# Paired tails of experts, projections by products of parts, and a later load of shared weights, in a two-layer float32 stack on one core

## The chip, the core and the metric

The kernel runs on one core of a Trainium2 chip. Such a core has a matrix engine (TensorE, PE in the profile, with its weight loads shown apart as PEld), three engines for elementwise work (VectorE or DVE, ScalarE or ACT, GpSimd or POOL), and SyncE (SP), which here only issues transfers. Each engine takes its own instructions in order; they wait for one another through semaphores. Data lies in SBUF (128 partitions) and PSUM (eight banks of 128 x 512 floats, into which TensorE writes). The metric is the device time of one execution in microseconds (us); lower is better.

## The reference

The reference is six blocks, each added to its input: windowed self-attention, cross-attention, a mixture of 64 experts with a shared expert, a state-space mixer, a second cross-attention and a dense layer with low-rank experts. There are 8 sequences of 256 tokens, width 512. The change touches the first three blocks. What matters of them:

```python
# self-attention: 16 heads, a window of 64 keys; its last step is the output projection
out = out.transpose(0, 2, 1, 3).reshape(B, S, EMB)
return out @ w_out.T
...
# cross-attention: its last projection, before a layernorm of the delta
ctx = ctx.transpose(0, 2, 1, 3).reshape(B, S, H)
delta = _nan_clean(ctx @ Wo.T + bo)
...
# experts: 192 places each; buf holds the rows routed to an expert
buf = jnp.zeros((E * C, H), x.dtype).at[slot].set(x[tok]).reshape(E, C, H)
g = jnp.einsum('ech,emh->ecm', buf, Wg)
u = jnp.einsum('ech,emh->ecm', buf, Wu)
out = jnp.einsum('ecm,ehm->ech', jax.nn.silu(g) * u, Wd).reshape(E * C, H)
...
shared = jax.nn.silu(x @ Sg.T) * (x @ Su.T) @ Sd.T
```

## The kernel before

Everything is written out by hand: each stage is a block in which every engine has its own program, and the order of the code is the order of the work. Waits are for constants of counts. There are four stages in a row: `phase1` (both attentions of the first layer, sequence by sequence), `shared_expert` (the shared expert, the router and the scatter of tokens into expert slots), `phase2` (the 64 experts), and then the second layer (`mixers`, `lora_ffn`), which the change leaves alone but for two semaphores that are taken from a reused range.

Two ways of multiplying float32 stand side by side. Either TensorE takes float32 operands directly (`project_pe`, L188), or each operand is first split into a high part, rounded to the format fp32r by an ACT copy, and a low part, the rest, by a DVE subtraction; the product is then the sum of three products of parts, high by high, high by low and low by high (`PRODUCTS`, issued by `products`, L730, in `phase1` and by L328 and L1797 for the experts).

**`phase1`.** Eight sequences, i from 0 to 7, one after the other; `last` is 7. For a sequence PE first projects queries and keys in eight chunks and the values (L730, `w_slot`), then runs the local heads (L780 to L822). DVE divides each chunk of 128 channels of attended values by its row sums into `oT` (`divide`, L1002), after ACT has copied the reciprocals (`copy_recips`, L626). PE covers the end of that with half of the cross values (`cross_values(0)`), multiplies `oT` by `w_out` in float32 (8 instructions of 128 x 512: two blocks j of 128 rows by four chunks; every one shows as two records in the trace), and goes on with `cross_values(1)`. DVE adds the result to the input (`residual`, L1007) and takes the statistics of the layernorm. In the cross-attention the divided values come as two halves (L1109), after two ACT copies (L711); PE covers these with the keys of the next sequence (`keys(i + 1, (3,))`) and then multiplies by `w_xo`, again in float32. DVE takes the two blocks of the delta (`take_delta`, L971) and turns at once to the rotary step (`rope`, L959 to L962) of the next sequence, which PE awaits before its first local scores (L780). The tiles `w_sg`, `w_su`, `w_sd` and `hr0` at the right end of SBUF hold raw pieces of projection weights in sequence 0 and are then free until the shared expert's weights are loaded into them, in sequence 2 (L524 to L532). In sequence 7 the splitting of those weights, the turning of the first rows of the next stage and its first products are laid between the cross-attention's steps (`shared_opening`, `shared_turn`, `shared_gate_up`).

**`phase2`.** For expert e PE runs gate and up (three chunks m of the 352 hidden channels, L328), turns the gathered rows of expert e + 1 (`turn_expert`, L302), and then multiplies down (L1797: for each m three products, in the order aT_hi by wd_hi, aT_hi by wd_lo, aT_lo by wd_hi; L1801 for the last 64 rows in float32). The 192 rows of an expert are gathered as two tiles, 128 and 64 rows, by two indirect transfers of POOL, and both tiles are turned as full 128 x 128 blocks: eight transposes, half of the second four's output unused. ACT and DVE split the turned rows (L308, L314). For each m DVE makes the gated activation (L1854, L1858), its high part aT_hi (L1861) and its low part aT_lo (L1863); PE waits for aT_lo (`eact_ready`) before the first of the three products of that m. Buffers are in twos by the parity b of e, and the raw down weights in fours.

## Time and profile before

| | us |
|---|---|
| time, median of 3 runs | 3115.08 (3113.67 to 3115.29) |
| time of the profiled execution | 3110.33 |
| its span | 3108.5 |
| `phase1`, sequences 0 to 7 | 0 to about 759 |
| one sequence of it | 90 to 92 |
| `shared_expert` | about 760 to 1001 |
| `phase2` | about 1001 to 1771 |
| one expert, in the steady part | about 12.1 |
| second layer | from there to 3108.5 |

The profiled execution took 1.8 us more than its span, and 4.75 us less than the median of the three timed runs. Over the whole span PE is busy 95%, DVE 74%, ACT 51% and POOL 26% of the time. A PE record starts where its matmul begins to stream and is longer than the time until the next one starts, since matmuls overlap; so the cost of a group is read from its first start to the first start of what follows.

### The profile page before, as it was taken

Reading aid. Unit: us, or ns where it says so; the run is one execution under the profiler, and the core shown is the slowest. Engines: PE = TensorE matmul, PEld = TensorE weight load, DVE = VectorE, ACT = ScalarE, POOL = GpSimd, SP = SyncE. Lnnn points to the kernel's source line nnn. Section 1 sums busy time; section 2 is a strip of 40 time slices with the busy share of each in tenths; the row PEclk is TensorE's granted clock in tenths of the full one; section 3 lists DMA queues with packets and bytes.
Section 4 is the critical chain, followed back from the end, with each engine's and each line's share of the span. In section 5 each row is a group of like instructions: output and inputs, shape, how many; then the busy total and the mean of one; then the engine's idle time right before and its main releaser. Section 6 shows DMA issues by size and latency. Waiting matters only on the chain. (4 is left out here: it accounts for less than half of the span.)

```text
span 3108.5 us, 61772 instructions
## 1 busy us (share of the span) xinstructions
PE 2954.8 (95%) x23073; PEld 2384.2 (77%) x23073; DVE 2301.0 (74%) x4321; ACT 1579.0 (51%) x3643; POOL 808.7 (26%) x974
## 2 busy tenths in 40 slices
PE   7999999998999999999999969999999989999999
PEld 5666666665998888888888846767676678888888
DVE  5665666665876788888888668878786887777776
ACT  3323333333222555555555436666666765555554
POOL 1221122122664111111111073342412022222222
PEclk9999999999999999999999989999999999999999
DMA  7324333330312777777777642221210032222222
GB/s 281 116 93 188 126 140 112 126 113 29 119 56 65 235 244 248 236 249 237 250 244 243 229 142 65 69 73 56 69 42 18 33 125 75 76 79 80 76 69 72
DMA packets 146539, 403.96 MB, mean 130 GB/s; under 512 B 39488, under 2 KB 48192, under 8 KB 133520
## 3 DMA queue, kind: packets, MB, share of 16 engines
q1 hardware_dynamic: 107888, 325.36, 30.8%
q0 software_dynamic: 18976, 50.45, 5.7%
q10 hardware_dynamic: 19456, 25.18, 2.4%
q8 instruction: 143, 2.34, 0.3%
q14 instruction: 76, 0.62, 0.1%
HBM read 344.06 MB, written 54.76 MB: 128 GB/s over the span
## 5 line engine op out<-in xcount | busy, mean ns | idle before, releaser
L288 POOL DMA_INDIRECT hr<-normed_rows,idx x128 | 124.4, 972 | 629.2 <-PE psum L302 593.0
L3018 POOL TENSOR_TENSOR mixf<-act 128x256 f32<-128x256 f32 x128 | 143.2, 1119 | 458.6 <-DVE act L3284 458.6
L174 POOL TENSOR_SCALAR ve<-mv 128x1 f32<-128x1 f32 x112 | 35.9, 321 | 762.7 <-DVE mv L967 505.5
L328 PE MATMUL psum<-xT_hi,wgu_hi 128*128 128x192 f32 (+1 forms) x1536 | 228.4, 271 | 1.5 <-PEq L1127 0.9
L328 PE MATMUL psum<-xT_hi,wgu_lo 128*128 128x192 f32 (+1 forms) x1536 | 223.3, 268 | 0.0
L328 PE MATMUL psum<-xT_lo,wgu_hi 128*128 128x192 f32 (+1 forms) x1536 | 223.1, 268 | 0.0
L1744 ACT ACTIVATE eth<-psum 128x192 f32<-128x192 f32 (+1 forms) x192 | 63.2, 330 | 300.2 <-PE psum L328 293.5
L328 PEld LDWEIGHTS psum<-xT_hi,wgu_hi 128*128 128x128 f32 (+1 forms) x1536 | 190.3, 182 | 26.7 <-ACT wgu_hi L1728 21.5
L2312 ACT ACTIVATE scratch<-psum,smin 128x512 f32<-128x512 f32 x256 | 173.7, 687 | 62.3 <-DVE smin L2758 60.6
L328 PEld LDWEIGHTS psum<-xT_lo,wgu_hi 128*128 128x128 f32 (+1 forms) x1536 | 190.7, 183 | 0.0
L328 PEld LDWEIGHTS psum<-xT_hi,wgu_lo 128*128 128x128 f32 (+1 forms) x1536 | 190.5, 183 | 0.0
L3284 DVE TENSOR_TENSOR act<-act,maskT 128x512 f32<-128x512 f32 x128 | 88.1, 689 | 116.7 <-ACT act L3060 116.3
L2758 DVE TENSOR_REDUCE smin<-psum 128x2 f32<-128x1024 f32 x128 | 155.2, 1215 | 25.3 <-PE psum L2489 24.5
L2499 PEld LDWEIGHTS psum<-ident,scratch 128*128 128x128 f32 x1024 | 109.2, 141 | 59.0 <-issue 37.7
L2499 PE MATMUL psum<-ident,scratch 128*128 128x128 f32 x1024 | 145.3, 281 | 7.5 <-DVE scratch L2765 3.9
L1854 DVE SCALAR_TENSOR_TENSOR eact<-eth,psum 128x192 f32<-128x192 f32 (+1 forms) x192 | 67.5, 352 | 113.2 <-ACT eth L1744 110.8
L3294 DVE TENSOR_TENSOR ca_lo<-act,ca_hi 128x512 fp32r<-128x512 f32 x128 | 134.3, 1049 | 12.4
L730 PE MATMUL psum<-hT_hi,w_slot 128*128 128x256 f32 x768 | 110.8, 289 | 11.9 <-ACT hT_hi L607 5.9
L1267 POOL DMA_INDIRECT slot_token<-tok_i,slot_w x96 | 103.4, 1077 | 66.5 <-DVE slot_r L1592 41.6
L1098 DVE TENSOR_SCALAR arena<-psum,hi 128x512 f32<-128x512 f32 x128 | 87.5, 745 | 42.9 <-PE psum L836 42.9
L2126 POOL DMA_INDIRECT yk<-expert_out,slots x84 | 86.3, 1028 | 119.8 <-issue 48.4
L3073 ACT ACTIVATE ca_hi<-act 128x512 fp32r<-128x512 f32 x128 | 81.0, 633 | 66.5 <-DVE act L3284 66.5
(466 smaller groups left out, 8644.4 us busy)
## 6 DMA issues: line engine op xcount, KB each, us to landing
w_sg<-in_w_gu_dram SPq DMA_DIRECT2D x32, 1408.0 KB, 6.0
w_su<-in_w_gu_dram SPq DMA_DIRECT2D x32, 1408.0 KB, 5.9
w_slot<-w_split SPq DMA_DIRECT2D x21, 2048.0 KB, 8.9
w_raw<-in_w_dram SPq DMA_DIRECT2D x128, 256.0 KB, 2.6
w_sd<-in_w_d_dram SPq DMA_DIRECT2D x32, 512.0 KB, 8.7
wd<-in_w_d_dram SPq DMA_DIRECT2D x32, 512.0 KB, 8.6
expert_out<-so ACTq DMA_DIRECT2D x64, 256.0 KB, 5.3
w_slot<-w_split SPq DMA_DIRECT2D x28, 512.0 KB, 5.0
```

Source lines behind the costliest of these rows:

```text
L288: pool.indirect_dma_start(out=xg[0:w, t, :], out_offset=None, in_=rows, in_offset=bass.IndirectOffsetOnAxis(ap=idx[0:w, t:t + 1], axis=0)) ...
L328: ins = pe.matmul(bank(2 + m)[0:w, gu * CAP:(gu + 1) * CAP], wgu2[wp][:, gu, kc, m0:m0 + w], xT2[xp][:, kc, :], start=(i == 0 and kc == 0) ...
L730: ins = pe.matmul(out, lhs_of(lp, kc), rhs_of(rp, kc), start=(m == 0 and kc == 0), stop=(m == 2 and kc == KC - 1))
L1098: dve.tensor_scalar(xprobs[:, n % 4, kt], bank_pair(2 * (n % 2))[:, :, kt * S:(kt + 1) * S], hi[:, kt:kt + 1], -SCORE_CLIP * ROOT_HD, ALU. ...
L1267: pool.indirect_dma_start(out=dr["slot_token"], out_offset=bass.IndirectOffsetOnAxis(ap=slot_w[s % 2][:, j, k:k + 1], axis=0), in_=tok_i[s ...
L2126: pool.indirect_dma_start(out=gathered(s, NT * k + j), out_offset=None, in_=dr["expert_out"], in_offset=bass.IndirectOffsetOnAxis(ap=slots ...
L2312: act.activation(prob[:, q % 4, k, :], bank_pair(2 * (q % 2))[:, k, :], ACT.Exp, bias=smin[b][:, n, k:k + 1], scale=-1.0, accum_out=ssum[b ...
L2499: ins = pe.transpose(bank(4 + k)[:, mc * P:(mc + 1) * P], prob[:, q % 4, k, mc * P:(mc + 1) * P], ident)
L2758: dve.tensor_reduce(smin[(q // PAIRS) % 2][:, q % PAIRS, :], bank_pair(2 * (q % 2)), AX.X, ALU.min).then_inc(sy["smin_ready"], 1)
L3018: pool.tensor_tensor(mixf[:, g % LAG, :], act2[:, g % LAG, 0, :], act2[:, g % LAG, 1, :], ALU.add).then_inc(sy["f_mix"], 1)
L3284: dve.tensor_tensor(act2[:, g % LAG], act2[:, g % LAG], maskT[(g // FC) % 2][:, 2:4, :], ALU.mult).then_inc(sy["f_ca"], 1)
L3294: dve.tensor_tensor(ca2[1][:, g % LAG], act2[:, g % LAG], ca2[0][:, g % LAG].bitcast(F32), ALU.subtract).then_inc(sy["f_ca_lo"], 1)
```

## The change

Three things change.

First, in the experts: an even expert e now gathers, as its second tile, its own last 64 rows and the last 64 rows of expert e + 1 (`load_slots`, `gather_expert`), and turns eight blocks; the odd expert gathers and turns only its first 128 rows, four blocks, and takes its last 64 from the half of bank 1 that its neighbour's turn left (`turned_tiles`). The down products wait for the high part before the first product of an m and for the low part only before the third.

Second, in sequences 1 to 6 of `phase1`: both output projections are done by products of parts. `w_out` and `w_xo` are split once, at the end of sequence 0, into tiles laid over `w_su`, `w_sd`, `hr0` and part of `w_sg`; `oT` is split for each projection by ACT (`attended_hi`, `crossed_hi`) and DVE (`low_part`) into tiles laid over `qk`. Sequences 0 and 7 stay in float32.

Third, since the split weights occupy the room, the shared expert's weights and its first rows are loaded in sequence 7, behind the load of the cross queries' weights.

```diff
 def load_slots(sp, sy, dr, idx, e, b):
-    sp.dma_start(idx[0:CAP - P, 1:2], slot_token[bass.ds(e * CAP + P, CAP - P)]).then_inc(sy[f"idx_in{b}"], 16)
+    for half in range(0 if b else 2):
+        sp.dma_start(idx[half * SMALL:(half + 1) * SMALL, 1:2],
+                     slot_token[bass.ds((e + half) * CAP + P, SMALL)]).then_inc(sy[f"idx_in{b}"], 16)
...
 def gather_expert(pool, sy, dr, xg, idx, b):
-    for t, (c0, w) in enumerate(C_TILES):
+    for t in range(1 if b else 2):
         pool.indirect_dma_start(
-            out=xg[0:w, t, :], out_offset=None, in_=rows,
-            in_offset=bass.IndirectOffsetOnAxis(ap=idx[0:w, t:t + 1], axis=0)).then_inc(sy[f"xg_in{b}"], 16)
+            out=xg[:, t, :], out_offset=None, in_=rows,
+            in_offset=bass.IndirectOffsetOnAxis(ap=idx[:, t:t + 1], axis=0)).then_inc(sy[f"xg_in{b}"], 16)
...
+def turned_tiles(bank, b):
+
+    tiles = [bank(t)[:, :].rearrange("p (c t) -> p c t", c=KC) for t in range(2)]
+    return (slice(0, P), tiles[0]), (slice(P, CAP), tiles[1][:, :, b * SMALL:(b + 1) * SMALL])
+
+def turn_expert(pe, sy, ident, bank, xg, b):
+    for t in range(1 if b else 2):
+        for kc in range(KC):
+            ins = pe.transpose(bank(t)[:, kc * P:(kc + 1) * P], xg[:, t, kc * P:(kc + 1) * P], ident)
     ins.then_inc(sy["exT_psum"], 1)
...
+        OUT_PARTS, XO_PARTS = ((0, 2), (2, 3), (3, 4)), ((0, 2), (2, 4))
+        def in_parts(i):
+
+            return 0 < i < last
...
-                if i == 2:
-                    sp.wait_ge(sy["rows_out"], i * 32)
+                else:
+                    sp.wait_ge(sy["delta_psum"], due("delta_psum", i - 1, NT))
+                    sp.wait_ge(sy["rows_out"], (i - 1) * 32)
+                    for n in ("w_sg", "w_su"):
+                        sp.dma_start(held[n][:], dr[n]).then_inc(sy["shared_in"], 16)
                     sp.dma_start(held["hr0"][:], dr["normed_rows"][0].rearrange("(t p) d -> p t d", p=P)
                                  ).then_inc(sy["shared_in"], 16)
...
+            def out_weights_hi(n, half):
+                act.wait_ge(sy["w_lo"], split_done(XQ, KC - 1))
+                kcs = slice(2 * half, 2 * half + 2)
+                act.activation(w_o2[n][0][:, kcs, :], W_RAW[n][:, kcs, :], ACT.Copy).then_inc(sy["w_hi"], 1)
...
                 copy_recips(i, 2)
+                if in_parts(i):
+                    attended_hi(i, 0)
                 copy_recips(i, 3)
+                if in_parts(i):
+                    attended_hi(i, 1)
+                    attended_hi(i, 2)
...
+                if in_parts(i):
+                    for part in range(len(XO_PARTS)):
+                        crossed_hi(i, part)
                 if i < last:
                     keys_copy(i + 1, 3, KC)
...
+            def out_products(out, n, j, first, end):
+
+                return products(out[:, :], lambda p, kc: oT2[p][:, kc, j * P:(j + 1) * P],
+                                lambda p, kc: w_o2[n][p][:, kc, :], PRODUCTS, first, end)
...
+                if in_parts(i):
+                    pe.wait_ge(sy["w_lo"], split_done(XQ, KC - 1) + 4)
+                    pe.wait_ge(sy["oT_hi"], xo_part(i, len(XO_PARTS)))
+                    for j in range(NT):
+                        out_products(bank(6 + j), "xo", j, 0, 2)
+                        if j == 0:
+                            pe.wait_ge(sy["oT_lo"], xo_part(i, len(XO_PARTS)))
+                        out_products(bank(6 + j), "xo", j, 2, 3).then_inc(sy["delta_psum"], 1)
...
+            def low_part(count, c0, end):
+                dve.wait_ge(sy["oT_hi"], count)
+                dve.tensor_tensor(oT2[1][:, c0:end, :], oT[:, c0:end, :], oT2[0][:, c0:end, :].bitcast(F32), ALU.subtract
+                                  ).then_inc(sy["oT_lo"], 1)
...
+                if i == 0:
+                    for k in range(4):
+                        out_weights_lo(k, ("out", "xo")[k // 2], k % 2)
...
                 for m in range(NM):
-                    pe.wait_ge(sy["eact_ready"], e * NM + (m + 1))
+                    pe.wait_ge(sy["ehi_ready"], e * NM + (m + 1))
                     for i, (ap, wp) in enumerate(PRODUCTS):
+                        if ap:
+                            pe.wait_ge(sy["eact_ready"], e * NM + (m + 1))
                         pe.matmul(bank(5)[:, :], aT2[b][ap][:, m, 0:P], wd2[b][wp][:, m, :],
                                   start=(m == 0 and i == 0), stop=(m == NM - 1 and i == 2))
```

How this stands in the program, in three places. In the lists `x8` means eight alike in a row, and the waits of an instruction stand behind it.

PE at the end of sequence 1 of `phase1`, before: the keys of the next sequence (ctxT by w_xk), the projection (w_xo), and the first queries of sequence 2.

```order
L188 MATMUL psum<-ctxT,w_xk 128x256 [waits colsT_lo]
L188 MATMUL psum<-ctxT,w_xk 128x256 x3
L188 MATMUL psum<-w_xo,oT 128x512 [waits xattn_ready]
L188 MATMUL psum<-w_xo,oT 128x512 x7
L730 MATMUL psum<-hT_hi,w_slot_76 128x256 [waits slot_a,xk_ready,colsT_lo]
```

PE at the same place now.

```order
L187 MATMUL psum<-ctxT,w_xk 128x256 x3
L788 MATMUL psum<-w_xo_hi,oT_hi 128x512 [waits oT_hi,w_lo]
L788 MATMUL psum<-w_xo_hi,oT_hi 128x512 x3
L788 MATMUL psum<-w_xo_lo,oT_hi 128x512 x4
L788 MATMUL psum<-w_xo_hi,oT_lo 128x512 [waits oT_lo]
L788 MATMUL psum<-w_xo_hi,oT_lo 128x512 x3
L788 MATMUL psum<-w_xo_hi,oT_hi 128x512 x4
L788 MATMUL psum<-w_xo_lo,oT_hi 128x512 x4
L788 MATMUL psum<-w_xo_hi,oT_lo 128x512 x4
L788 MATMUL psum<-hT_hi,w_slot_80 128x256 [waits slot_a,xk_ready,colsT_lo]
```

Eight float32 instructions have become 24 of parts; the first now waits for ACT's copy of `oT` and the ninth for DVE's low part.

ACT over the cross-attention's end in sequence 1, before: xkT is the copy of keys, cosq and sinq take the spread reciprocals.

```order
L615 ACTIVATE xkT<-psum,bk 128x256 [waits xk_psum]
L711 ACTIVATE cosq<-psum 128x512 [waits xrecT_psum]
L711 ACTIVATE sinq<-psum 128x512 [waits xrecT_psum]
L615 ACTIVATE xkT<-psum,bk 128x256 [waits xk_psum]
L663 ACTIVATE arena<-psum 128x256 [waits qk_proj] x8
```

ACT at the same place now.

```order
L646 ACTIVATE xkT<-psum,bk 128x256 [waits xk_psum]
L762 ACTIVATE cosq<-psum 128x512 [waits xrecT_psum]
L762 ACTIVATE sinq<-psum 128x512 [waits xrecT_psum]
L673 ACTIVATE oT_hi<-oT 128x512 [waits xattn_ready] x2
L646 ACTIVATE xkT<-psum,bk 128x256 [waits xk_psum]
L709 ACTIVATE arena<-psum 128x256 [waits qk_proj] x8
```

The two copies of `oT` stand between the copy of the second reciprocals and that of the last keys.

PE in `phase2`, within an even expert, between its gate and up products and the rest of its down products, before: hr is the odd neighbour's gathered rows.

```order
L302 MATMUL psum<-ident,hr_85 128x128 [waits exT_lo,xg_in1]
L302 MATMUL psum<-ident,hr_85 128x128 x7
L1797 MATMUL psum<-wd_hi_96,aT_hi_108 128x512 [waits eact_ready,eout_ready,wd_lo]
L1797 MATMUL psum<-wd_lo_97,aT_hi_108 128x512
L1797 MATMUL psum<-wd_hi_96,aT_lo 128x512
L1797 MATMUL psum<-wd_hi_96,aT_hi_108 128x512 [waits eact_ready]
```

PE at the same place now.

```order
L316 MATMUL psum<-ident,hr_89 128x128 [waits exT_lo,xg_in1]
L316 MATMUL psum<-ident,hr_89 128x128 x3
L1900 MATMUL psum<-wd_hi_100,aT_hi_112 128x512 [waits ehi_ready,eout_ready,wd_lo]
L1900 MATMUL psum<-wd_lo_101,aT_hi_112 128x512
L1900 MATMUL psum<-wd_hi_100,aT_lo 128x512 [waits eact_ready]
L1900 MATMUL psum<-wd_hi_100,aT_hi_112 128x512 [waits ehi_ready]
```

Four of the eight transposes are gone at this one of the two places in a pair of experts, and the wait for the low part stands two products later.

## Rows read from the trace of the kernel before

**Rows 1.** The page's part 1: busy time, share of the span, instructions.

```profile
PE 2954.8 (95%) x23073; PEld 2384.2 (77%) x23073; DVE 2301.0 (74%) x4321; ACT 1579.0 (51%) x3643; POOL 808.7 (26%) x974
```

**Rows 2.** Busy time and granted clock in five stretches; columns in the first row.

```profile
core 0: us, PE busy (x) PEld busy (x) DVE busy (x) ACT busy (x) POOL busy (x), PEclk, DMA share, GB/s
...
322.00:327.00 5.00, 5.00 (x25) 3.60 (x22) 2.53 (x5) 2.90 (x16) 0.00 (x0) 0.66 0.33 124
...
392.00:483.00 91.00, 87.04 (x716) 59.41 (x715) 58.01 (x100) 32.57 (x100) 18.07 (x25) 1.00 0.33 119
...
727.00:736.00 9.00, 8.47 (x65) 4.48 (x66) 5.53 (x9) 6.68 (x9) 1.27 (x1) 0.62 0.00 0
...
1040.00:1766.00 726.00, 726.00 (x6061) 644.49 (x6060) 593.26 (x1081) 403.69 (x660) 112.54 (x118) 1.00 0.75 248
```

**Rows 3.** PE's timeline, sequence 3: start, length, instruction, [idle before].

```profile
346.52 7.03 PE L188 MATMUL psum<-w_out,oT 128*128 128x512 f32 x16
353.39 3.60 PE L188 MATMUL psum<-w_xv,ctxT 128*128 128x512 f32 x8
...
389.20 7.03 PE L188 MATMUL psum<-w_xo,oT 128*128 128x512 f32 x16
395.66 1.50 PE L730 MATMUL psum<-hT_hi,w_slot 128*128 128x256 f32 x8
```

**Rows 4.** PE's timeline, sequence 7: values of one block as products of parts.

```profile
683.25 2.13 PE L730 MATMUL psum<-w_slot,hT_hi 128*128 128x512 f32 x8
...
686.16 0.39 PE L780 MATMUL psum<-wmask_b,ident_b 128*128 128x256 bf16 x2
```

**Rows 5.** DVE's timeline, sequence 3, then durations of splits (min/median/max ns).

```profile
343.70 0.43 DVE L1002 TENSOR_TENSOR oT<-psum,rec 128x256 f32<-128x256 f32 x1 [0.75 <-ACT rec L626]
...
388.30 0.69 DVE L1109 TENSOR_TENSOR oT<-psum,sinq 128x512 f32<-128x512 f32 x1 [0.17 <-ACT sinq L711]
...
396.27 0.75 DVE L971 SCALAR_TENSOR_TENSOR so<-psum,rs,rs_bo 128x512 f32<-128x512 f32 x1 [1.74 <-PE psum L188]
...
L632 ACT ACTIVATE sg_hi<-w_sg x6: 406/615/622, 728.3 to 751.6; 128x512 fp32r<-128x512 f32 x5, 128x256 fp32r<-128x256 f32 x1
L1019 DVE TENSOR_TENSOR sg_lo<-w_sg,sg_hi x6: 421/686/691, 728.9 to 756.4; 128x512 fp32r<-128x512 f32 x5, 128x256 fp32r<-128x256 f32 x1
```

**Rows 6.** End of sequence 0 on ACT and DVE, and splits of 128 x 1024.

```profile
118.39 0.47 ACT L615 ACTIVATE xkT<-psum,bk 128x256 f32<-128x256 f32 x1 [1.13 <-PE psum L188]
...
125.25 0.75 DVE L971 SCALAR_TENSOR_TENSOR so<-psum,rs,rs_bo 128x512 f32<-128x512 f32 x1 [1.74 <-PE psum L188]
...
L1734 ACT ACTIVATE wd_hi<-wd x32: 1049/1052/1056, 1020.1 to 1760.9; 128x1024 fp32r<-128x1024 f32 x32
...
L1831 DVE TENSOR_TENSOR wd_lo<-wd,wd_hi x32: 1224/1226/1228, 1021.7 to 1762.5; 128x1024 fp32r<-128x1024 f32 x32
```

**Rows 7.** One expert's turn and down products: PE's timeline, then DVE's.

```profile
1511.18 1.04 PE L302 MATMUL psum<-ident,hr 128*128 128x128 f32 x8
1511.98 0.48 PE L1797 MATMUL psum<-wd_hi,aT_hi 128*128 128x512 f32 x1
...
1513.46 0.39 PE L1797 MATMUL psum<-wd_hi,aT_hi 128*128 128x512 f32 x1
...
1512.51 0.26 DVE L1861 CAST aT_hi<-eact 96x192 fp32r<-96x192 f32 x1
1512.80 0.35 DVE L1863 TENSOR_TENSOR aT_lo<-eact,aT_hi 96x192 fp32r<-96x192 f32 x1
```

**Rows 8.** PE's waits from 1000 to 1050: us in total, times, longest.

```profile
PE psum L1797 <- DVE aT_lo L1863: 3.6, 4, 1.6
```

**Rows 9.** Transfers: shared weights' time to land, SP and PE in sequence 7.

```profile
w_sd<-in_w_sd_dram SPq DMA_DIRECT2D x1, 128.0 KB, 18.2
...
688.45 0.59 SPq L473 DMA_DIRECT2D w_slot<-w_split  x1
...
725.72 0.66 PE L182 MATMUL psum<-ident,hr 128*128 128x128 f32 x4
```

More of the change, by code:

```diff
@@ L213, in shared_weights @@
     tiles = {n: right(n, shape) for n, shape in shapes.items()}
+    at = nc.sbuf_top
+    tiles["w_o2"] = {n: [nc.alloc_sbuf_tensor_at(f"w_{n}_{part}", [P, KC, D], F32R, offset=at + 4 * (2 * i + j) * KC * D)
+                         for j, part in enumerate(("hi", "lo"))] for i, n in enumerate(("xo", "out"))}
     tiles["w_gate"] = ctx.enter_context(nc.sbuf_tensor("w_gate", [P, KC, E], F32))
@@ L362, in phase1 @@
         wmask = arena[:, 2048:2048 + S]
+        qk_at = nc.sbuf_base
         qk = sb("qk", [P, 2 * KC, S])
+        oT2 = [nc.alloc_sbuf_tensor_at(f"oT_{part}", [P, KC, S], F32R, offset=qk_at + 4 * j * KC * S)
+               for j, part in enumerate(("hi", "lo"))]
         xkT = sb("xkT", [P, KC, S])
@@ L716, in _ @@
                     shared_chunks_hi(4, len(MS_CHUNKS))
+                if i == 0:
+                    for n in ("out", "xo"):
+                        for half in range(2):
+                            out_weights_hi(n, half)
             sy.end_turn(act, 0, 0)
@@ L1073, in _ @@
                 divide(i, 2)
+                if in_parts(i):
+                    low_part(out_part(i, 1), *OUT_PARTS[0])
                 divide(i, 3)
+                if in_parts(i):
+                    for part in (1, 2):
+                        low_part(out_part(i, part + 1), *OUT_PARTS[part])
                 if i == 0:
@@ L1111, in _ @@
                                       ALU.mult).then_inc(sy["xattn_ready"], 1)
+                if in_parts(i):
+                    for part in range(len(XO_PARTS)):
+                        low_part(xo_part(i, part + 1), *XO_PARTS[part])
+                if i == 0:
+                    for k in range(4):
+                        out_weights_lo(k, ("out", "xo")[k // 2], k % 2)
             for at in range(4, 9):
@@ L1634, in _ @@
             dve.wait_ge(sy["exT_hi"], 1)
-            turned_lo(dve, sy, bank, first["xT2"])
+            turned_lo(dve, sy, bank, first["xT2"], 0)
             out(nseq - 1)
```

121 lines of the change are left out of this document (71 added, 50 removed).

## The prediction

> **What bounds the kernel now.** I read the busy shares first [rows 1]: PE is busy 95% of the span, DVE 74%, ACT 51%. Then the busy time by stretches [rows 2], since such a share is a mean over stages. In the steady part of the experts PE is busy 726.0 of 726 us at full clock: every TensorE instruction taken out there counts, unless a wait takes its place. In a sequence of `phase1` (392 to 483 is sequence 4) PE is busy 87 of 91 us, and there the question is what it waits for after the edit. So the third view is PE's timeline around the projections and the turn [rows 3, 4, 7], beside DVE's and ACT's at the same moments [rows 5 to 7]. I cost each edit as a change of PE's time, and then look at whether its inputs would come in time.
>
> **The local output projection, sequences 1 to 6.** Before, w_out takes from 346.52 to 353.39, 6.87 us, for 8 float32 instructions (16 records) [rows 3]. The same shape as products of parts is there in the values: 12 products, from 683.25 to 686.16, 2.91 us [rows 4]. The new projection has 24 of them, 5.82 us, so it saves 1.05. Its inputs: the last chunk of oT is ready at 343.70 + 0.43 = 344.13 [rows 5]; ACT copies it as 128 x 256 (0.41, the shortest of the sg_hi copies), DVE subtracts (0.42) [rows 5], and both are done by about 345.1, while PE comes there at 346.52. The first low part is issued between two divisions, where DVE idled 0.75 us [rows 5], about its own length. DVE and ACT have nothing to do until the first block of the projection is out, so nothing waits behind these splits. The second block is out 1.05 earlier, and the layernorm and the turning that hang on it move along. 6 x 1.05 = 6.3 us.
>
> **The cross projection, same sequences.** The same 1.05 is saved: w_xo's records are as long and as many as w_out's [rows 3]; its next start comes after 6.46 and not 6.87, but the group that starts there is stretched to 1.50 us, and I take it that the missing 0.4 is in it. Here the inputs are late. The second half of oT ends at 388.30 + 0.69 = 388.99, and PE starts at 389.20. Now ACT's copy of 128 x 512 stands between, 0.615 us [rows 5]. With 0.1 for two hand-overs, my allowance, PE starts at 389.7, 0.5 late. Bounds of that: 0.4 with no hand-overs, and 0.8 with two of 0.2, which is what DVE takes after PE (396.27 against 389.20 + 6.87). I take 0.5, since the shorter hand-overs are those between ACT and DVE. DVE's second low part would end at about 390.4, PE needs it after eight products, at 391.6: hidden. Queued behind ACT's new copies is only the copy of the last keys, for which PE asks after the projection; behind DVE's is the delta, not out before 392.6. The second delta block is out at 395.5 and not at 396.1, so both PE's queries and DVE's long run through layernorm and rotation, for which PE waits before the local scores, start 0.55 earlier. 6 x 0.55 = 3.3 us, within 1.5 and 3.9.
>
> At this place a rule of the Trainium skill stands against the row. The row has a float32 instruction of 512 columns at 6.87 / 8 = 0.86 us and a product of parts at 2.91 / 12 = 0.243 [rows 3, 4]. The Trainium skill (FP8 and Floating Point Precision, section TensorE Precision Notes) says that true float32 takes four passes through the array, and reduced precision is a matter of one read and truncation; by that rule three products would take three quarters of 6.87, and the saving would be 1.72 and not 1.05. The trace agrees with the four passes only in part, since its product is 13% dearer than a quarter of 0.86; the rule's own time is among the rivals.
>
> **Splitting the two weights, once, end of sequence 0.** ACT is free from 118.39 + 0.47 = 118.9 and makes four copies of 128 x 1024, 1.05 each, until 123.1; its next work comes after that. DVE follows with four subtractions of 1.23, from about 119.9 to 124.8 [rows 6]. They stand before the delta in its queue. The first block (about 1.6 us with its statistics) then ends near 126.4, and the second starts there and not at 125.25 [rows 6]: 1.2 us late, and it is that run for which PE waits before the scores. Cost 1.2 us, once; between 0 (if its slack takes it) and 1.5.
>
> **The turn of the experts.** Eight transposes take from 1511.18 to 1511.98, 0.80 us [rows 7]. The 32 turns of odd experts keep four, so each saves 0.40. That the products behind can start earlier needs their inputs. The third m's first product, at 1513.46, would stand at 1513.06. Its high part is ready at 1512.51 + 0.26 = 1512.77; its low part at 1512.80 + 0.35 = 1513.15, too late for the old wait, and in time for the new one, since the third product comes two products later, near 1513.5. DVE's work up to there starts from the gate's results and is not moved. Extra waits that are already met should cost nothing. 32 x 0.40 = 12.8 us. From below 0.25 a turn, 8.0 us, if PE can start the third m only as if the low part were still asked for (the distance from 1513.21, the low part with a hand-over, to 1513.46); from above 0.45, 14.4 us, as the group's own length of 1.04 hints. The even turns have as many transposes as before. ACT's and DVE's splits keep their 768 columns, cut as 512 and 256. POOL has 32 gathers less, of the same rows in all.
>
> **The opening of the experts.** SP issues a third index transfer ahead of expert 2's weights, about 0.5 us, and PE's four waits for low parts, 3.6 us [rows 8], may each shrink by up to 0.35 through the later wait. I take 0, within 1.5 either way.
>
> **The shared weights.** In sequence 2 they stood, as they will in sequence 7, right behind a load of 2 MB of projection weights, and the last of them landed 18.2 us after its issue. In sequence 7 they can be issued from 689.0 on, so they are there by about 709 to 711; PE turns their first rows at 725.72 [rows 9]. Some 15 us to spare, cost nothing. If that cover were gone the delay would come whole onto the path, since PE and ACT both wait for them. Taking them out of sequence 2 gives nothing that I can see.
>
> **The clock.** The granted clock is 1.00 in sequence 4 and in the experts; from 322 to 327, in sequence 3, it is 0.66 and from 727 to 736, in sequence 7, 0.62, that is, 1.2 GHz for most of these stretches [rows 2]. These cost 5 x 0.34 = 1.7 and 9 x 0.38 = 3.4 us. Sequence 4 has the same work as sequence 3, leaves PE idle for 4 us too and stays at 1.00, so I can't say where dips will fall in the new kernel. I allow 4 us either way and take 0.
>
> **Sum.** 6.3 + 3.3 - 1.2 + 12.8 = 21.2 us less. The profiled execution, 3110.33, would be 3089.1. It stood 4.75 below the median of the timed runs, so for the median I take 3115.08 - 21.2 = **3093.9 us**.
>
> **The rivals.**
> - *The down products still wait at the short turns.* For it: only 0.3 us lie between the high part and the new start. Against: DVE's chain is that early by the row. The turn then saves 8.0: 3098.7 us. 10%.
> - *The cross projection gains nothing,* because ACT and DVE come later than in my one sequence, or the 0.5 us spreads. 3115.1 - 17.9 = 3097.2 us. 10%.
> - *The dips of the clock go.* For it: they look like chance. Five us more gain: 3088.8 us. 10%.
> - *Three quarters,* the float32 pass's share and nothing for the weight loads. 12 x 0.67 = 8.0 us more: 3085.9 us. The values' row speaks against it. It is the rule named above. 4%.
> - *The turn is hidden,* that is, the experts are paced by arriving weights or by DVE (82% busy there), and only `phase1` gains, 8.4: 3106.7 us. Against: PE's 726.0 of 726. 4%.
> - *Slower.* The new wait before each cross projection and the shorter, denser local one bring a low clock after them, as after the light stretches of rows 2, at 3.4 us each. With all twelve: 40.8 - 21.2 = 19.6 us more, 3134.7 us. It decides from seven of the twelve on (21.2 / 3.4 = 6.2). Against: sequence 4 has 4 us of waits already and no dip [rows 2]. 4%.
>
> **How the numbers follow.** My forecast has 58%, with 3090 to 3097 as its own range. The range for 8 in 10 takes in the first three rivals and most of the unknown costs, and leaves out the last three (12%) and the tails: 3087 to 3102. A measurement of this kernel tells about 0.2%, 6.2 us, from no change. Faster by more than that is everything below 3108.9: all but the slow rival and a few per cent around the hidden turn, 93%; within it 3%; slower 4%.
>
> **What would show it.** In the new profile: the span from w_out's first start to the cross values behind it is 5.8 us; PE idles about 0.5 us before w_xo, put down to ACT, in sequences 1 to 6 only; the short turn takes 0.40 and a pair of experts 23.8 and not 24.2 us, with no wait for the high or the low part behind it; PE's wait before sequence 1's scores is about 1.2 us longer; nothing waits for the shared weights in sequence 7. Wrong would be: PE idle before the down products of even experts, an idle of 1 us or more before w_xo, the wait for `qk` before the scores longer by what the projections save, or new stretches of clock under 0.7.

## The result, and the profile after

The changed kernel takes 3093.92 us (median of 5 runs, 3090.02 to 3101.35) where the kernel before, beside it on the same chip, takes 3115.08 (5 runs, 3113.67 to 3116.58): a ratio of 0.9933, 95% interval 0.9917 to 0.9949. Measured again beside the experiments it took 3088.78 us against 3112.29, a ratio of 0.9927 (0.9915 to 0.9939). The forecast was 3093.9.

So the total is right. That the first median meets it to a tenth is luck: its five executions spread over 11 us, and the second median is 5 us lower. Its parts are not all right, and that is what the rest is about. The profiled execution took 3093.92 us, span 3092.2, which is 16.4 less than the profiled execution of before, where the sum said 21.2. The changed kernel's page, part 1, to be read beside [rows 1]:

```profile
PE 2935.5 (95%) x23041; PEld 2391.8 (77%) x23041; DVE 2315.3 (75%) x4355; ACT 1597.6 (52%) x3677; POOL 779.7 (25%) x940
```

Five stretches of the changed kernel in the view that [rows 2] has of before; the number behind POOL's is the granted clock:

```profile
core 0: us, PE busy (x) PEld busy (x) DVE busy (x) ACT busy (x) POOL busy (x), PEclk, DMA share, GB/s
142.50:149.30 6.80, 6.80 (x26) 4.59 (x26) 2.84 (x5) 3.00 (x17) 0.00 (x0) 0.50 0.41 155
...
323.50:326.90 3.40, 3.40 (x15) 2.49 (x11) 2.23 (x5) 2.65 (x15) 0.00 (x0) 0.51 0.09 31
422.40:432.60 10.20, 9.92 (x94) 6.66 (x94) 3.50 (x7) 4.06 (x22) 0.00 (x0) 0.50 0.77 326
497.00:588.00 91.00, 86.59 (x757) 64.81 (x755) 63.25 (x111) 35.74 (x107) 20.70 (x31) 1.00 0.35 127
1040.00:1750.00 710.00, 709.88 (x5907) 627.46 (x5907) 583.50 (x1074) 399.97 (x656) 85.41 (x87) 1.00 0.74 252
```

The experts are as they were, full clock and PE busy throughout, only shorter. In sequences 1 to 6 of `phase1` there are now stretches at 1.2 GHz (a granted clock of 0.50) in sequences 1, 2, 3 and 4, 23.9 us together with the 3.4 us from 234.7; before there was one, 3.4 us in sequence 3.

The undisturbed sequence 5 of the changed kernel on PE, for [rows 3], from its first scores to the queries of the next sequence:

```profile
504.46 0.38 PE L843 MATMUL psum<-wmask_b,ident_b 128*128 128x256 bf16 x2 [0.82 <-DVE qk L1044]
...
525.75 3.60 PE L187 MATMUL psum<-w_xv,ctxT 128*128 128x512 f32 x8
528.79 1.49 PE L788 MATMUL psum<-w_out_hi,oT_hi 128*128 128x512 f32 x4
...
534.76 3.59 PE L187 MATMUL psum<-w_xv,ctxT 128*128 128x512 f32 x8
538.19 1.04 PE L181 MATMUL psum<-ident,so 128*128 128x128 f32 x8
...
568.85 1.89 PE L187 MATMUL psum<-ctxT,w_xk 128*128 128x256 f32 x8
571.18 1.17 PE L788 MATMUL psum<-w_xo_hi,oT_hi 128*128 128x512 f32 x4 [0.44 <-ACT oT_hi L673]
...
576.83 1.10 PE L788 MATMUL psum<-hT_hi,w_slot 128*128 128x256 f32 x8
```

The eight float32 instructions of `w_xv` take 3.43 us for half a projection (534.76 to 538.19), so the local projection starts at 525.75 + 3.43 = 529.18 and lasts until 534.76: 5.58 us, 0.2325 a product. (Its first record already starts at 528.79, but the next one comes only 0.63 us later. Both groups together take 9.01 us, and took 10.30 before, so the saving doesn't hang on where the border is laid.) The cross projection takes 5.65 and starts 0.60 late (571.18, where the keys would have let it start at 568.85 + 1.73 = 570.58). From the first cross values of sequence 5 to those of sequence 6 it is 87.92 us; before, 89.81.

A short turn and the down products behind it, for [rows 7], and the first long turn after it:

```profile
1510.56 0.60 PE L316 MATMUL psum<-ident,hr 128*128 128x128 f32 x4
1510.92 0.48 PE L1900 MATMUL psum<-wd_hi,aT_hi 128*128 128x512 f32 x1
...
1512.39 0.40 PE L1900 MATMUL psum<-wd_hi,aT_hi 128*128 128x512 f32 x1
...
1513.18 1.51 PE L1904 MATMUL psum<-wd,eact 128*64 128x256 f32 x12
...
1522.22 1.03 PE L316 MATMUL psum<-ident,hr 128*128 128x128 f32 x8
1523.02 0.48 PE L1900 MATMUL psum<-wd_hi,aT_hi 128*128 128x512 f32 x1
```

The short turn takes 0.36 us, the long one 0.80, and nothing waits behind these two. At others something does: between 1100 and 1700 us PE's weight loads wait 13 times for the high part, up to 0.5 us.

```profile
PEld psum L1900 <- DVE aT_hi L1964: 3.9, 13, 0.5
```

PE's waits from 140 to 700 us (us in total, times, longest):

```profile
PE psum L843 <- DVE qk L1044: 7.7, 7, 2.8
...
PE psum L788 <- ACT oT_hi L673: 2.6, 6, 0.4
...
PE psum L877 <- DMA v_mid<-v: 1.2, 1, 1.2
```

The wait of 2.8 us before the scores is that of sequence 1, behind the splitting of the weights; its six others are 0.4 to 1.2 us, as in the kernel before. The wait for `v_mid`, the shifted values, is in sequence 4, and its long stretch of low clock begins at 422.44, at the end of that wait (PE's timeline):

```profile
422.68 0.66 PE L877 MATMUL psum<-arena,v 128*32 128x128 f32 x8 [1.22 <-DMA v_mid<-v]
```

Where the 16.4 us lie, by the starts of the same instruction in both profiles: 1.3 us before the first cross projection, where nothing was changed; 0.8 from there to the router's first product (645.28 and 644.48 us); 0.1 in `shared_expert`; 15.0 from the first expert's gate to the second layer (813.71 and 798.70 us); and 0.9 lost again in the second layer. So `phase1`, for which the sum had 8.4, gave almost nothing in this execution. Two things hide in it: the projections gave more than forecast, and the splitting of the weights and the low clock took it back.

### The profile page after: what moved, and what is told of

The parts are those of the page before. It is cut to its first block and busy times, and to the rows that moved or that the text cites. A ratio compares the mean times of both kernels' runs of the same rounds, so it can differ in the third digit from the quotient of the medians.

```text
span 3092.2 us, 61813 instructions
## 1 busy us (share of the span) xinstructions
PE 2935.5 (95%) x23041; PEld 2391.8 (77%) x23041; DVE 2315.3 (75%) x4355; ACT 1597.6 (52%) x3677; POOL 779.7 (25%) x940
## 5 line engine op out<-in xcount | busy, mean ns | idle before, releaser
L292 POOL DMA_INDIRECT hr<-normed_rows,idx x96 | 95.8, 998 | 642.3 <-PE psum L316 597.1
L3397 DVE TENSOR_TENSOR ca_lo<-act,ca_hi 128x512 fp32r<-128x512 f32 x128 | 134.2, 1048 | 12.5
```

Of the source, the lines that this page charges most:

```text
L292: pool.indirect_dma_start(out=xg[:, t, :], out_offset=None, in_=rows, in_offset=bass.IndirectOffsetOnAxis(ap=idx[:, t:t + 1], axis=0)).the ...
L3397: dve.tensor_tensor(ca2[1][:, g % LAG], act2[:, g % LAG], ca2[0][:, g % LAG].bitcast(F32), ALU.subtract).then_inc(sy["f_ca_lo"], 1)
```

## The experiments

All are read against the kernel before on the same chip. Since every kernel's time moved by several us with the mean granted clock of the execution, I also give the span that a straight line through all executions' spans against their mean clocks gives for a clock of 0.987. The line has one slope for all kernels, 2.3 us for each 0.001, and a height for each; single executions lie 1.4 us about it. Differences under 2 us between its values should not be leant on. "At equal clock" below means these values.

| kernel | median us | runs | ratio (95%) | mean clock | span at 0.987 |
|---|---|---|---|---|---|
| before | 3112.8 | 63 | | 0.9863 | 3109.3 |
| changed, both measurements | 3090.3 | 11 | 0.9933, 0.9927 | 0.9854 | 3086.4 |
| late_load | 3113.1 | 11 | 0.9999 (0.9991 to 1.0008) | 0.9858 | 3108.9 |
| late_wait | 3111.9 | 11 | 1.0000 (0.9991 to 1.0009) | 0.9862 | 3108.6 |
| parts_only | 3109.6 | 12 | 0.9992 (0.9983 to 1.0001) | 0.9845 | 3102.3 |
| tails_only | 3098.9 | 6 | 0.9951 (0.9938 to 0.9965) | 0.9868 | 3097.3 |
| xo_parts | 3101.6 | 5 | 0.9958 (0.9945 to 0.9971) | 0.9852 | 3095.1 |
| wout_parts | 3090.6 | 5 | 0.9923 (0.9910 to 0.9936) | 0.9868 | 3088.5 |
| old_wait | 3108.2 | 11 | 0.9983 (0.9974 to 0.9992) | 0.9839 | 3098.9 |
| filled | 3087.6 | 5 | 0.9920 (0.9907 to 0.9934) | 0.9880 | 3088.5 |
| split_later | 3094.8 | 5 | 0.9941 (0.9927 to 0.9954) | 0.9844 | 3087.5 |
| late_add | 3084.6 | 5 | 0.9907 (0.9894 to 0.9921) | 0.9866 | 3079.5 |
| v123 | 3077.1 | 4 | 0.9886 (0.9872 to 0.9901) | 0.9873 | 3076.3 |

In what follows a dip is a stretch of granted clock 0.50. My theory of the dips went through three forms, and the letters in the expectations change with it. In the first four, A is chance and B is that the denser projections and longer waits bring the dips. In the next ones A is what B was, narrowed to the cross projection, and C is chance. Last came the idle time before the scores.

**One part alone: tails_only.** The kernel before with the expert hunks of the diff.

> The kernel before with the experts' part of the change alone: paired tails, 32 short turns of four transposes, and the later wait for the low part. Both theories, the edits add up and only their sizes are open: in the profile of the changed kernel the short turn took 0.36 us and a pair of experts 23.78 to 23.86 us for 24.2 before, so 29 pairs of steady experts give some 11.5 us, and the opening of the experts 1.3 more through the later wait: 3115.1 - 13 = 3102. If the experts were paced by something else behind PE, under 5 us.

Measured 3098.87. At equal clock 12.0 us, where some 13 were expected. 56 intervals from turn to turn take 666.41 us in its profile against 677.76.

**The other part alone: parts_only.** The kernel before with all other hunks.

> The kernel before with both projections of sequences 1 to 6 by parts and the later load of shared weights, experts as before. Theory A, the dips of the clock fall by chance: a sequence without a dip takes 87.9 us for 89.8, so 6 x 1.9 - 1.7 for the splitting of the weights = 9.7 us less, 3105.4 us, and its mean clock is not lower than that of the kernel with the later load alone. Theory B, the denser projections and the longer waits bring the dips: the net gain is about 1 us as between the two profiles (dips 11.8 us in sequences 1 to 4 against 1.6), 3114 us, with a mean clock some 0.003 to 0.005 lower.

Measured 3109.56: between A and B, and not clear of no gain at all (the interval reaches 1.0001). At equal clock it gains 6.7 us on late_load, and its mean clock is lower by 0.0013, some 3 us.

Two things in it don't fit a plain sum. Its experts, whose code is that of before, take 679.65 us for the 56 intervals, 1.9 more than before and than late_load (677.73), and between 1100 and 1700 us PE's weight loads wait more often for the low part (in the kernel before it is 1.4 us in 8 waits):

```profile
PEld psum L1891 <- DVE aT_lo L1957: 4.1, 13, 0.6
```

And at equal clock the two parts give 12.0 and 7.0, where the whole change gives 22.9. Of the 3.9 us between, one lies in the experts, where the whole takes 0.9 us more than tails_only and not 1.9; the rest, some three times the uncertainty of this sum, is open.

**late_load.** As parts_only, with this edit and without the splitting of `w_out` and `w_xo`:

```diff
         def in_parts(i):
 
-            return 0 < i < last
+            return False
```

> The kernel before with only the load of the shared expert's weights and first rows moved from sequence 2 to sequence 7; projections in float32, experts as before. Expected by the sum: no cost, 3115.1 us within 1, and no wait for the shared weights. If the load is late or disturbs other transfers, 1 us or more slower. It also shows how often the clock dips in float32 sequences.

Measured 3113.11 against 3113.04. The later load costs nothing. Its profile has dips in sequences 3, 5 and 6: float32 sequences have them too.

**wout_parts.** The changed kernel with the cross projection in float32.

```diff
-                if in_parts(i):
+                if False:
                     pe.wait_ge(sy["w_lo"], split_done(XQ, KC - 1) + 4)
...
-                if in_parts(i):
-                    for part in range(len(XO_PARTS)):
-                        crossed_hi(i, part)
```

> The changed kernel with the cross projection in float32 again (w_xo's parts are still made, not used). Theory A: it loses what the cross projection gave, 6 x 0.62 = 3.7 us, 3097.6 us. Theory B, the wait for ACT's copy before w_xo and what follows it bring the dips: the loss is made up by fewer dips, 3094 us or less, with a mean clock above 0.986.

Measured 3090.59 at a mean clock of 0.9868: by its numbers that is theory B, and I took the dips for the cross projection's fault. An undisturbed sequence takes 88.54 us, so this projection gives 1.27 of the 89.81.

**after_again and xo_parts.** The changed kernel once more, and with the local projection in float32 instead.

> The changed kernel once more, beside the three below. From the runs so far, a line through spans against mean clocks puts it at 3087.0 us of span for a mean clock of 0.987, where the kernel before stands at 3109.3; its mean clock was 0.9846 in five executions, that of the kernel before 0.9861 in 23. Theory A (the cross projection by parts lowers the clock): again 0.9845 or so and 3094 us. Theory C (it was chance): a mean clock of 0.986 and 3090 us.

Measured 3088.78, clock 0.9860 in six executions. That is theory C's number, and the median, 1.8 us under that of wout_parts, is not told from it. So the low clock of the first five was in part chance. That all of it was is not shown.

> The changed kernel with the local projection in float32 again, the cross projection still by parts. At equal clock it should lose the local projection's gain, 6 x 1.29 = 7.7 us, and stand near 3094.7 us of span for a clock of 0.987. Theory A: its mean clock is as low as the changed kernel's, 0.9845, so the median is near 3102 us, slower than the experts' part alone (3098.9). Theory C: clock as in the kernel before, median near 3098.

Measured 3101.60 at a mean clock of 0.9852: the median is theory A's. An undisturbed sequence takes 89.24 us, so the cross projection gives 0.57; with 1.27 that makes 1.84 of the 1.89 that both give.

**late_add.** The changed kernel with DVE's additions moved off the path to the scores. GpSimd's matching work moves with them, and SP now loads the cross queries' weights and shifts the values before it stores the last sequence's rows; of these hunks only DVE's is shown:

```diff
                 for n in range(KC):
                     rope(i, n)
...
-                    if i >= 1 and n == 0:
+                    if i >= 1 and n == KC - 1:
                         for j in range(NT):
                             add_delta(i - 1, j)
```

> The changed kernel with VectorE's two additions of the normalised delta and their statistics (3.3 us) behind the fourth rotary step instead of the first, GpSimd's matching work and the store behind them too. PE's wait before the local scores (0.82 us in a sequence, 2.8 in sequence 1) should go: 6 to 8 us less at equal clock. Theory A in its form that this wait brings the dips: the mean clock rises from 0.9845 to 0.9865, 4 us more, about 3084 us. If the dips have another source: about 3087 us with the clock still at 0.9845. If the wait only moves to another place behind: 3092 or more.

Measured 3084.59, with 3079.5 at equal clock: 7 us better than the changed kernel. An undisturbed sequence takes 87.18, and in sequences 1 to 6 of the profile no dip is left. That profile is the fastest of five executions (3074.75 us, mean clock 0.989); the slowest had 0.984, so other executions had more low clock somewhere. Sequence 1, and sequences 2 to 6, of the changed kernel and then of late_add:

```profile
131.00:172.00 41.00, 36.74 (x331) 25.69 (x329) 27.36 (x53) 17.06 (x77) 6.61 (x10) 0.92 0.41 156
180.00:690.00 510.00, 484.13 (x4148) 359.17 (x4147) 345.40 (x590) 200.04 (x587) 106.68 (x146) 0.98 0.33 118
```

```profile
131.00:172.00 41.00, 39.00 (x358) 28.05 (x357) 29.67 (x58) 17.41 (x78) 8.42 (x13) 1.00 0.48 167
180.00:690.00 510.00, 489.13 (x4302) 360.80 (x4302) 349.03 (x604) 206.64 (x623) 96.75 (x142) 1.00 0.38 131
```

**filled.** late_add takes the wait away and DVE's chain with it. This one leaves the chain and fills PE's wait:

```diff
             def scores(i, n):
+                if i >= 1 and n == 0:
+                    for k in range(6):
+                        pe.matmul(bank_pair(0)[:, k % 2, 0:S], ident_b[:], wmask_b[:], start=True, stop=True)
```

> The changed kernel with six throwaway products (bf16, 128x256, about 0.16 us each) before PE's wait for the rotary step in sequences 1 to 7: they fill the 0.4 to 1.3 us of idle time there, and shorten nothing. If the idle time itself brings the dips of the clock in sequences 1 to 6, none is left there (the kernel that took the wait away had none, the changed kernel had four in one profile and two in the other): a sequence takes 87.9 to 88.1 us and the median is 2 to 4 us under the changed kernel's 3089 to 3094. If the dips come from something else that late_add took away, they stay at 2 to 4 and the median is the changed kernel's or up to 2 us above.

The six products are extra work, overwritten by what follows. Measured 3087.62, with the highest mean clock of all, 0.9880: its five executions have 0.987 to 0.989, the changed kernel's eleven 0.981 to 0.987. In time nothing is shown by that, since its ratio, 0.9920, lies within the changed kernel's intervals, and at equal clock it stands 2 us above the changed kernel. Its sequences 2 to 6 have no dip; sequence 1, where 1.81 us of wait remain in front of the scores, has one:

```profile
131.00:172.00 41.00, 37.51 (x339) 26.44 (x338) 27.79 (x52) 17.10 (x77) 7.22 (x10) 0.92 0.44 163
180.00:690.00 510.00, 488.13 (x4293) 362.84 (x4294) 350.47 (x600) 205.04 (x615) 106.68 (x146) 1.00 0.35 124
```

Over all profiles, sequences 2 to 6: with the wait before the scores in place there are 8 dips in 25 float32 cross projections (before 1, late_load 3, late_wait 2, tails_only 2, wout_parts 0) and 13 in 30 by parts; without it, or filled, 0 in 15. Of the 21, 19 begin 1.2 to 2.8 us after the first scores, and the other two, in sequence 4 of the changed kernel and sequence 3 of xo_parts, begin at the end of a wait of 1.2 us for `v_mid`. So PE's idle time goes with the dips. That it brings them is what filled speaks for, since it only fills the idle time; its profile alone (0 of 5 where the others have 21 of 55) would come by chance once in eleven times, and its clocks over five executions are the stronger evidence.

The projections by parts have a share in it that the count of dips doesn't show, 8 of 25 against 13 of 30. All 8 last 3.4 us; of the 13, five last 6.8 or 10.2. And over all executions changed, parts_only and xo_parts, which have the cross projection by parts and the wait before the scores, have a mean clock of 0.9850 in 28 executions (old_wait and split_later, lower still, add waits of their own). The five kernels with this projection in float32 have 0.9863 in 96, wout_parts with its 0.9868 among them; late_add, v123 and filled, which have the parts and not the wait, come to 0.9873 in 14. So parts and wait together go with 0.0013 less, some 3 us, four times its uncertainty. In what way the parts act is not shown.

**old_wait.** The changed kernel with the experts' wait where it was.

```diff
-                    pe.wait_ge(sy["ehi_ready"], e * NM + (m + 1))
+                    pe.wait_ge(sy["eact_ready"], e * NM + (m + 1))
                     for i, (ap, wp) in enumerate(PRODUCTS):
-                        if ap:
-                            pe.wait_ge(sy["eact_ready"], e * NM + (m + 1))
```

> The changed kernel with the experts' old wait: PE asks for the low part already before the first of the three products. By the rows of the kernel before, the low part is there 0.25 us after the point at which the short turn now ends earlier, so each of 32 short turns gives 0.25 and not 0.40: a pair of experts 23.95 us, some 4.5 us more than the changed kernel, with a wait for the low part behind each short turn. The rival: the low part comes in time at the short turns too and the later wait only helps in the opening: 1 us more.

Measured 3108.24, 12.5 us above the changed kernel at equal clock. The 56 intervals take 678.60 us: no less than the 677.76 of the kernel before, and 1.05 less than the 679.65 of parts_only, from which it differs by the paired tails alone (3 us at equal clock). PE's timeline at a short turn, and then DVE's at the third m:

```profile
1522.72 0.60 PE L316 MATMUL psum<-ident,hr 128*128 128x128 f32 x4
1523.08 0.48 PE L1898 MATMUL psum<-wd_hi,aT_hi 128*128 128x512 f32 x1
...
1524.32 0.40 PE L1898 MATMUL psum<-wd_hi,aT_lo 128*128 128x512 f32 x1
1524.74 0.50 PE L1898 MATMUL psum<-wd_hi,aT_hi 128*128 128x512 f32 x1
1525.08 0.40 PE L1898 MATMUL psum<-wd_lo,aT_hi 128*128 128x512 f32 x1
...
1525.64 0.66 PE L1902 MATMUL psum<-wd,eact 128*64 128x256 f32 x4
```

```profile
1524.34 0.35 DVE L1964 TENSOR_TENSOR aT_lo<-eact,aT_hi 96x192 fp32r<-96x192 f32 x1
```

The low part ends at 1524.69 and PE starts at 1524.74, 0.18 after 1524.32 + 0.24. Then the first product after the wait takes 0.34 to the next, and not 0.23. Both together are 0.29 of the 0.43 us that the turn saved, and waits at some long turns and longer pairs (up to 25.60 us) take the rest. Of the waits from 1040 to 1760 us most stand at PE's weight load and few at PE, so the list for PE alone would have shown a sixth of them:

```profile
PEld psum L1898 <- DVE aT_lo L1964: 19.7, 36, 1.3
...
PE psum L1898 <- DVE aT_lo L1964: 4.1, 14, 0.9
```

**late_wait.** The kernel before with only that wait moved.

> The kernel before with the later wait alone, eight transposes everywhere. No wait for the low part stands in the steady experts before, so nothing changes there: 24.2 us a pair. In the opening four waits sum to 3.6 us and may shrink by up to 0.35 each: 0 to 1.4 us less, within the measurement, 3112.

Measured 3111.93. The later wait gives nothing alone, and without it the short turns give 1 to 3 us: the gain is the pair's.

**split_later.** The changed kernel with the weights' low parts made by GpSimd in sequence 1.

```diff
-                if i == 0:
-                    for k in range(4):
-                        out_weights_lo(k, ("out", "xo")[k // 2], k % 2)
...
+                if i == 1:
+                    for k in range(4):
+                        pool.wait_ge(sy["w_hi"], split_done(XQ, KC - 1) + k + 1)
+                        n, kcs = ("out", "xo")[k // 2], slice(2 * (k % 2), 2 * (k % 2) + 2)
+                        pool.tensor_tensor(w_o2[n][1][:, kcs, :], W_RAW[n][:, kcs, :],
+                                           w_o2[n][0][:, kcs, :].bitcast(F32), ALU.subtract).then_inc(sy["w_lo"], 1)
```

> The changed kernel with one edit: the low parts of the two projection weights are made by GpSimd within sequence 1's heads, where it is idle, instead of by VectorE at the end of sequence 0. In the seven profiles so far that have this splitting on VectorE, PE waits 1.8 to 2.9 us before sequence 1's scores and the clock dips right behind it in every one, for 3.4 to 10.2 us; in the four without the splitting and in the two where the wait is gone it never does. Theory: the splitting's true price is the 1.7 us of the wait and 1.7 to 5.1 us of low clock behind it, so this kernel is 3 to 6 us faster than the changed one, about 3085 to 3088 us, sequence 1 without its dip. Rival: the dip in sequence 1 has nothing to do with the longer wait; then only 1.7 us are gained and the dip is still there.

Measured 3094.76: the expectation failed, and the profile says why. POOL's, PE's and DVE's timelines at that place:

```profile
140.69 5.16 POOL L609 TENSOR_TENSOR w_out_lo<-w_out,w_out_hi 128x1024 fp32r<-128x1024 f32 x2
```

```profile
140.51 0.38 PE L849 MATMUL psum<-wmask_b,ident_b 128*128 128x256 bf16 x2 [1.01 <-DVE qk L1050]
...
148.68 0.58 PE L849 MATMUL psum<-wmask_b,ident_b 128*128 128x256 bf16 x2 [2.88 <-ACT probs L729]
```

```profile
139.67 0.69 DVE L1050 TENSOR_TENSOR qk<-cosq,sinq 128x512 f32<-128x512 f32 x1
...
141.26 2.33 DVE L1048 TENSOR_TENSOR sinq<-sinq,sinT 128x512 f32<-128x512 f32 x1
143.62 2.78 DVE L1050 TENSOR_TENSOR qk<-rec,sinq 128x512 f32<-128x512 f32 x1
146.32 1.27 DVE L1151 TENSOR_REDUCE lmin<-psum 128x4 f32<-128x512 f32 x2
147.52 3.85 DVE L160 TENSOR_SCALAR so<-so,mv,rstd 128x512 f32<-128x512 f32 x2
```

The wait before the scores is down to 1.01 us and has no dip behind it. But beside POOL's subtractions DVE's steps with SBUF inputs take 2.33 and 2.78 instead of 0.69, so the scores' minima come late and PE waits 2.88 us eight microseconds on; there, from 148.49, the clock goes low for 23.9 us. The wait and its dip moved together. In all seven profiles with the splitting on DVE and the wait left in front of sequence 1's scores (1.8 to 2.9 us) there is a dip of 3.4 to 10.2 us, and in four of them (after_again, parts_only, xo_parts, old_wait) it begins 0.2 to 0.9 us before the first scores, within the wait; in the four without the splitting there is none in that sequence.

**v123.** late_add, the splitting as in split_later, and PE begins the cross projection on the first half of `oT`:

```diff
-                    pe.wait_ge(sy["oT_hi"], xo_part(i, len(XO_PARTS)))
+                    pe.wait_ge(sy["oT_hi"], xo_part(i, 1))
                     for j in range(NT):
-                        out_products(bank(6 + j), "xo", j, 0, 2)
+                        for kc in range(KC):
+                            if j == 0 and kc == 2:
+                                pe.wait_ge(sy["oT_hi"], xo_part(i, 2))
+                            pe.matmul(bank(6 + j)[:, :], oT2[0][:, kc, j * P:(j + 1) * P], w_o2["xo"][0][:, kc, :],
+                                      start=(kc == 0), stop=False)
+                        out_products(bank(6 + j), "xo", j, 1, 2)
```

> The kernel late_add with two more edits: PE starts the cross projection on the first two chunks as soon as the first half of oT is copied, so that its 0.6 us wait goes in each of six sequences (3 us), and the low parts of the two weights are made by GpSimd in sequence 1 instead of VectorE at the end of sequence 0, so that sequence 1's extra wait (1.7 us) goes: some 4 us less than late_add at equal clock. If DVE or the transfers set the time between the projection and the scores, the 3 us come back as a wait there and only 1 to 2 us are left.

Measured 3077.11, 1.1% under the kernel before and the best of all; at equal clock it is 3 us under late_add, for the 4 expected. A sequence takes 86.60 us, 0.58 less than late_add's: the wait for the copy is gone from PE's list. Here POOL's subtractions start later and meet DVE's reductions and copies of PSUM, which keep their 0.6 to 0.7 us each:

```profile
143.18 1.26 DVE L1156 TENSOR_REDUCE lmin<-psum 128x4 f32<-128x512 f32 x2
144.35 0.99 DVE L160 TENSOR_SCALAR so<-so,mv,rstd 128x512 f32<-128x512 f32 x2
146.77 0.69 DVE L1156 TENSOR_REDUCE lmin<-psum 128x4 f32<-128x512 f32 x1 [1.42 <-PE psum L856]
```

```profile
145.37 4.66 POOL L609 TENSOR_TENSOR w_out_lo<-w_out,w_out_hi 128x1024 fp32r<-128x1024 f32 x2
```

## Why the prediction was right, and where it was not

- **The local projection** was sized at 1.05 us and gives 1.29 (6.87 - 5.58). The term that was mis-sized is the product's price: 2.91 / 12 = 0.243, read from a group in the values that begins with a longer product, against 0.2325 in a run of 24. The Trainium skill (FP8 and Floating Point Precision, section TensorE Precision Notes) has four passes for float32, which would have given 1.72; the measured product is 8% dearer than a quarter of 0.86, so the rule's rival fell, but not by as much as I had it.
- **The cross projection** was sized at 0.55 and gives 0.62 beside the other, 0.57 alone. The wait was 0.60 late (forecast 0.5), and the cheaper product made up for it. v123 shows that the wait itself was avoidable.
- **The splitting** was sized at 1.2 us and costs 1.7: from the first cross projection to sequence 1's scores it is 24.10 us, before it was 22.43. I had bounded it at 1.5. What failed here is a term that I put at nothing without a reason: the clock behind a wait of 2.8 us in front of light work. The heads behind it took 24.34 us for 21.28: 3.1 us more. So the edit's price was near 4.7.
- **The turn** was sized at 0.40 and gives 0.43, but some pairs run longer and 28 pairs save 10.45 us (677.76 and 667.31), 0.37 each. The middle of the range was right. "No wait for the high or the low part behind it" was not, by the 3.9 us above. The bound was wrong: with the old wait I had 8.0 us left of 12.8, and old_wait against parts_only shows 1 to 3, since a late low part costs its lateness and a slower restart and some pairs wait longer.
- **The opening** was 0, within 1.5. From the first gate product to the first product of `wd` it is 43.84 us before and 40.34 after; 1.7 of the 3.5 are a shorter dip, and the other profiles scatter between 37.4 and 42.3, with late_wait alone at 39.8. I can't divide it further.
- **The shared weights** cost nothing, as forecast; late_load shows it apart.
- **The clock** was 0 within 4 us either way. In the first pair of profiles it cost 8.5: the changed kernel has 27.3 us of dips between the first cross projection and the router, the kernel before 10.2 (3.4 and 6.8), and half of the difference is lost. Taken out, that stretch gives 640.2 - 630.9 = 9.3 us against the 8.4 forecast. Over all executions the mean clock fell by 0.0009, which at 2.3 us for 0.001 is 2 us. New stretches under 0.7 were among my own signs of being wrong, and they are there: the allowance of 4 us holds over the executions and not in the first profile, and the zero in the middle was no reading of a row.

So the forecast of 21.2 stands on a gain at equal clock of 22.9 (3109.3 - 3086.4) less some 2 us of clock. Two errors met, and that they cancel is luck: the products were priced too high, and the clock was not priced at all. Of the rivals, the slower one had the right mechanism in part, a low clock brought on by a new wait, but laid it behind the projections, twelve times. What the runs show is one certain place, the scores of sequence 1, at some 3 us, and longer dips now and then at the scores of the others, where the wait is an old one. The profiles' difference of 16.4 against the medians' 21.2 has a plain reason: the profiled execution of before was among its fast ones.

## What to carry to other kernels

Price a wait on PE twice, by its length and by the clock behind it: 1.7 us more of wait in front of light matmuls cost 3.1 more in low clock. Filling the wait with six throwaway products raised the mean clock, but no gain in time is shown for it; making the awaited work come sooner gave 7 us at equal clock. When one engine's work is shortened, move the next engine's waits with it; the short turns gave some 12 us with the later wait and 1 to 3 without. When work is given to GpSimd to relieve VectorE, look at what VectorE runs beside it.

## What the runs showed of the hardware

- Idle time of 0.4 to 1.3 us before the light scores was followed by a dip to 1.2 GHz in 19 of 55 sequences, and not in the three profiles where it was taken away or filled (0 of 15). The other two dips in these sequences' heads began at the end of a wait of 1.2 us for a late transfer. With a wait of 1.8 to 2.9 us there was a dip in 7 of 7.
- The time of one and the same kernel spread over 12 us (before: 3105.68 us at a mean clock of 0.988, 3118.03 at 0.984).
- VectorE's 128x512 steps with two SBUF inputs went from 0.69 to 2.33 and 2.78 us, and its scaling of 128x512 from 0.50 to 1.9, beside GpSimd subtractions of 2.6 us each; its reductions from PSUM kept 0.6 to 0.7. The Trainium skill (SBUF — State Buffer, section Who interferes with whom) says that the SBUF ports shared by the two engines are an exclusive lock, that a DVE instruction with two SBUF inputs contends with a GpSimd instruction that reads SBUF, and that a reduction doesn't on trn2. The trace agrees: each of the two long steps lasted about as long as one of GpSimd's, and the reductions kept their time.
- The first product of 128x512 of a run took 0.34 us until the next one started, both after a wait (1524.74 in old_wait) and behind the scores' products with no wait (683.25 in the kernel before); after the transposes it took 0.31 to 0.32, and within a run 0.23.
